# A gated convolution block on one core: order of the opening changed, and one transpose for the last 32 channels of four tiles

## What is computed

```python
xn = srms(x)                          # x over its root mean square, by pixel
u = silu(xn @ u_w.T + u_b)            # 288 channels
v = silu(xn @ v_w.T + v_b)            # 288 channels
# a[288 channels, 128 offsets]: two small networks (3 layers of 256) of the offset
out = toeplitz_columns(v, a2) + toeplitz_rows(v, a1)    # in the reference by FFT
return (u * out) @ o_w.T + o_b + x
```

## Time and profile before

| | us |
|---|---|
| median of 3 runs | 752.12 |
| the three runs | 749.59, 752.12, 756.20 |
| the profiled execution | 749.46 |
| its span, first to last instruction | 747.7 |
| phase A, to | 148 |
| C0, to | 295 |
| body0, to | 507 |
| C1, to | 645 |
| body1, to | 748 |

### The profile page before, as it was taken

The page is one execution under the profiler, slowest core; times in us unless marked ns, Lnnn a source line. Parts: engine busy times, 40 slices in busy tenths (PEclk is TensorE's granted clock), DMA queues, the critical chain, the costliest instruction groups (busy, mean ns, idle before and its releaser), DMA issues.

```text
span 747.7 us, 19150 instructions
## 1 busy us (share of the span) xinstructions
PE 725.0 (97%) x7190; PEld 671.3 (90%) x7190; DVE 479.3 (64%) x863; ACT 528.3 (71%) x862; POOL 275.8 (37%) x184
## 2 busy tenths in 40 slices
PE   6899999999999998999999999999999999999998
PEld 6899899999999998899999999998999999887886
DVE  8477756258989898454444455445545455888887
ACT  4566678867767675778777778775767767676775
POOL 3233343112111213555554555511000000598984
PEclk9999999999999999999999999999999999999999
DMA  8755565499889985688888888869564656699996
GB/s 201 199 170 170 170 175 178 173 260 208 170 200 201 199 197 180 186 282 265 264 271 270 265 284 263 271 209 219 134 157 118 157 126 135 209 298 322 334 333 198
DMA packets 132308, 161.15 MB, mean 216 GB/s; under 512 B 69772, under 2 KB 97420, under 8 KB 132236
## 3 DMA queue, kind: packets, MB, share of 16 engines
q1 hardware_dynamic: 131948, 160.15, 76.6%
q10 hardware_dynamic: 288, 0.00, 0.0%
HBM read 109.49 MB, written 50.63 MB: 214 GB/s over the span
## 4 chain that ended last, share of the span: by engine, by line
PE 83%; DVE 8%; DMA 5%; issue 2%; SPq 1%; ACT 1%; POOL 0%; DVEq 0%; POOLq 0%; ACTq 0%
PE ps L1055 23%; PE ps L1162 17%; PE ps L1078 10%; PE ps L1068 10%; PE ps L1147 9%; PE ps L1134 8%; PE ps L1044 3%; DMA x_e<-in_x_eT 3%; PE ps L1081 2%; DVE toepB L903 2%; DMA free_rows<-in_x 1%; DVE r_diag L756 1%; DMA stage<-a_dram 1%; PE ps L1023 1%; DVE n_tmp L724 1%
## 5 line engine op out<-in xcount | busy, mean ns | idle before, releaser
L541 POOL TENSOR_TENSOR u_in<-u_in,v 128x1152 f32<-128x1152 f32 (+2 forms) x67 | 175.0, 2622 | 139.4 <-DMA u_in<-u_dram 132.2
L954 DVE TENSOR_TENSOR g<-ps,g 128x512 fp32r<-128x512 f32 (+1 forms) x192 | 125.4, 680 | 45.2 <-ACT g L614 42.2
L1162 PE MATMUL ps<-toepB,vt 128*128 128x128 f32 x1152 | 138.6, 278 | 0.2 <-DVE toepB L903 0.2
L1162 PEld LDWEIGHTS ps<-toepB,vt 128*128 128x128 f32 x1152 | 131.5, 192 | 6.8 <-ACT vt L650 6.1
L903 DVE COPY toepB<-stage 64x512 f32<-64x512 f32 x144 | 108.9, 756 | 43.4 <-PE ps L1162 40.1
L1055 PE MATMUL ps<-wv,xh 97*128 97x288 f32 x512 | 118.4, 307 | 5.4 <-DVE xl L811 5.2
L1055 PE MATMUL ps<-wu,xh 97*128 97x288 f32 x512 | 121.9, 303 | 0.0
L811 DVE TENSOR_TENSOR xl<-ps,xh 96x512 fp32r<-96x512 f32 x64 | 43.6, 682 | 108.5 <-ACT xh L586 108.4
L1068 PE MATMUL ps<-ident,u_in 128*128 128x128 f32 (+1 forms) x768 | 99.7, 272 | 3.1 <-DVE g L954 1.7
L1078 PE MATMUL ps<-g,wo 128*96 128x512 f32 x384 | 101.9, 400 | 0.0
L590 ACT ACTIVATE v<-ps 128x576 f32<-128x576 f32 (+1 forms) x128 | 83.4, 652 | 22.8 <-PE ps L1055 10.0
(11 more groups left out here) (84 smaller groups left out, 1015.4 us busy)
## 6 DMA issues: line engine op xcount, KB each, us to landing
stage<-a_dram SPq DMA_DIRECT2D x144, 256.0 KB, 4.6
u_in<-u_dram SPq DMA_DIRECT2D x64, 576.0 KB, 5.3
u_dram<-u_out SPq DMA_DIRECT2D x48, 576.0 KB, 3.3
x_e<-in_x_eT SPq DMA_DIRECT2D x64, 192.0 KB, 4.2
out<-x_e SPq DMA_DIRECT2D x64, 192.0 KB, 3.9
u_dram<-u_in SPq DMA_DIRECT2D x16, 576.0 KB, 2.9
x_n<-in_x SPq DMA_DIRECT2D x16, 384.0 KB, 5.8
xa<-in_x SPq DMA_DIRECT2D x64, 96.0 KB, 4.5
```

The lines of the kernel that those rows point to most:

```text
L541: return nc.gpsimd.tensor_tensor(out=tile, in0=tile, in1=v[:, start // 2:end // 2, bass.ds(t * NB, NB)].rearrange("p c n e -> p n c e"), o ...
L954: nc.vector.tensor_tensor(out=low, in0=ps[0:w, bank], in1=high.bitcast(f32), op=ALU.subtract).then_inc(gl_ready, 1)
L1162: last = nc.tensor.matmul(ps[:, SET_BANK[n % 2] + c // NB, (c % NB) * P:(c % NB + 1) * P], vt[n % 2][:, c], toepB[half][n % 2][:, c], star ...
```

## The change

1. **Opening.** ACT: `high_x(0, 0)` goes ahead of the squares of chunk 1. DVE: `low_x(1, 1)` goes ahead of the sum of chunk 1's squares. POOL: in the first chunk all four squares of chunk 2 are issued in step 3 (before: one in step 2, three in step 3).
2. **Networks.** PE issues `rpe_spreads` behind pair 3 of step 2 instead of behind pair 1.
3. **Joints.** DVE: `set_x_rows(0)` two units earlier. PE: in step 0 of body0 pair 2 ahead of the transposes of block 2. SP: at the end of body0 `load_xe` ahead of `load_stage`.
4. **body0, block 2.** POOL gates channels 0 to 255 in place and the last 32 of all four tiles into a new tile u_rest [128 tokens, 4 x 32], in a second instruction. PE transposes u_rest at once: one transpose 128x128, whose row is 32 n + channel. ACT copies the four groups of 32 rows to rows 0 to 31 of g[:, 4], each into its tile's columns (4 x 32x128); DVE copies each to rows 64 to 95 and subtracts into rows 32 to 63 (8 x 32x128). L1081 waits for all of it by two more semaphores. Half 1 keeps the old way.

The core of the diff:

```diff
@@ sync, body of phase_b0 @@
-                        if t >= STEPS - 2:
-
-                            sp.wait_ge(y_transposed, NCH * t)
-                            load_stage(1, t - (STEPS - 2))
                         if not first or r >= 2:
                             sp.wait_ge(o_stored[0][r % 2], 32 * c + 16 * (r // 2))
                             load_xe(0, t, r)
+                        if t >= STEPS - 2:
+
+                            sp.wait_ge(y_transposed, NCH * t)
+                            load_stage(1, t - (STEPS - 2))
@@ gpsimd @@
-                        for k in (((), (), (0,), (1, 2, 3)) if first else ((), (0,), (1,), (2, 3)))[r]:
+                        for k in (((), (), (), (0, 1, 2, 3)) if first else ((), (0,), (1,), (2, 3)))[r]:
                             square_a0(c + 2, k)
...
+                target = tile
+                if half == 0 and start == EARLY:
+                    target = u_rest[:, r % CH].rearrange("p (n c e) -> p n c e", n=NB, e=2)
...
-                        gate(0, t + 1, r + 1, c + 1 + (r + 1) // CH).then_inc(ug_ready, 1)
+                        loads = c + 1 + (r + 1) // CH
+                        gate(0, t + 1, r + 1, loads, 0, EARLY)
+                        gate(0, t + 1, r + 1, loads, EARLY, D).then_inc(ug_ready, 1)
@@ scalar @@
+            def high_rest(t, bank):
+
+                act.wait_ge(y_transposed, NCH * t + NCH)
+                wait(act, o_projected, t)
+                for n in range(NB):
+                    nc.scalar.copy(tile_columns(g[0:KW[2], 4], n), rest_of(ps[:, bank], n)).then_inc(gh_ready, 1)
+
...
+            high_x(0, 0)
             squares_of(x_chunk(1), x_sq1[:], 1)
-            high_x(0, 0)
@@ vector @@
+            low_x(1, 1)
             dve.wait_ge(opening_squared, 2)
             sum_opening(CH, CH, x_sq1[:])
-            low_x(1, 1)
...
-                    if half == 0 and n == UNITS - 1:
+                    if half == 0 and n == UNITS - 3:
                         set_x_rows(0)
...
+            def low_rest(t, bank):
+
+                w = KW[2]
+                for n in range(NB):
+                    dve.wait_ge(gh_ready, (2 + NB) * t + 2 + n + 1)
+                    nc.vector.tensor_copy(tile_columns(g[2 * w:3 * w, 4], n), rest_of(ps[:, bank], n)).then_inc(g_second, 1)
+                    low = nc.vector.tensor_tensor(out=tile_columns(g[w:2 * w, 4], n), in0=rest_of(ps[:, bank], n),
+                                                  in1=tile_columns(g[0:w, 4], n).bitcast(f32), op=ALU.subtract)
+                    low.then_inc(gl_ready if n == NB - 1 else g_low, 1)
@@ tensor @@
+                if half == 0 and k == NCH - 1:
+
+                    nc.tensor.transpose(ps[:, bank, 0:P], u_rest[:, r % CH], ident[:]).then_inc(y_transposed, 1)
+                    return
...
+                        if half == 0:
+                            pe.wait_ge(g_second, NB * (m + 1))
+                            pe.wait_ge(g_low, (NB - 1) * (m + 1))
                         nc.tensor.matmul(ps[0:E, bank], wo[0:REST + 2, 4], tile[0:REST + 2, 4],
...
-                if c <= LAYERS and r == 2:
-                    rpe_spreads(c)
...
+                    if c <= LAYERS and r == 2:
+                        rpe_spreads(c)
...
+                    if start:
+                        project(1, xs, r, 2)
                     transpose_g(0, t, r, 2, banks[2], NCH * t + 1)
-                    project(1, xs, r, 2)
+                    if not start:
+                        project(1, xs, r, 2)
```

More of the change, by code:

```diff
@@ L165, in tno_kernel, with rest_of, tile_columns @@
         assert base + K + 8832 <= nc.sbuf_usable_end
+        def rest_of(source, n):
+            return source[KW[2] * n:KW[2] * (n + 1), 0:P].rearrange("p (i c) -> p i c", i=2)
+        def tile_columns(rows, n):
+            return rows.rearrange("p (s i q c) -> p s q i c", s=2, i=2, q=2)[:, n // 2, n % 2]
         def u_tile(half, r):
@@ L412, in body @@
                             load_xa(t + 3, r + 1)
+                        if not first or r >= 2:
+                            sp.wait_ge(o_stored[0][r % 2], 32 * c + 16 * (r // 2))
+                            load_xe(0, t, r)
                         if t >= STEPS - 2:
@@ L540, in gate @@
                 tile = u_in[:, r % CH, :, start:end].rearrange("p n (c e) -> p n c e", e=2)
+                target = tile
+                if half == 0 and start == EARLY:
+                    target = u_rest[:, r % CH].rearrange("p (n c e) -> p n c e", n=NB, e=2)
                 return nc.gpsimd.tensor_tensor(
-                    out=tile, in0=tile, in1=v[:, start // 2:end // 2, bass.ds(t * NB, NB)].rearrange("p c n e -> p n c e"),
+                    out=target, in0=tile, in1=v[:, start // 2:end // 2, bass.ds(t * NB, NB)].rearrange("p c n e -> p n c e"),
                     op=ALU.mult)
@@ L689, in body0 @@
                             silu_v(1, t, pair)
-                    high_g(t, 2, banks[2], g, t)
+                    high_rest(t, banks[2])
                     for pair in range(2):
@@ L946, in set_rows, with gh_before, low_g @@
                     nc.vector.memset(tile[REST:REST + 2, 4].bitcast(f32), 1.0).then_inc(g_rows_set, 1)
-            def low_g(m, k, bank, tile):
-                dve.wait_ge(gh_ready, (NCH + 1) * m + (k + 1 if k < 2 else k + 2))
+            def gh_before(half, t):
+                return (2 + NB) * (t if half == 0 else STEPS) + (NCH + 1) * (t if half else 0)
+            def low_rest(t, bank):
[6 more added lines that the diff above has]
+                    low.then_inc(gl_ready if n == NB - 1 else g_low, 1)
+            def low_g(half, t, k, bank, tile):
+                dve.wait_ge(gh_ready, gh_before(half, t) + (k + 1 if k < 2 else k + 2))
                 w = KW[k]
@@ L1069, in transpose_g, with project_out @@
                 last.then_inc(y_transposed, 1)
-            def project_out(m, tile, bank, free, which=range(NCH)):
+            def project_out(half, m, tile, bank, free, which=range(NCH)):
                 for k in which:
@@ L1214, in body0 @@
                         pe.wait_ge(wo_split, 6)
-                    project_out(t, g, O_BANK, t, range(2))
+                    project_out(0, t, g, O_BANK, t, range(2))
                     project(1, xs, r, 3)
-                    project_out(t, g, O_BANK, t, (2,))
+                    project_out(0, t, g, O_BANK, t, (2,))
             def body1(c, first, last):
@@ L1231, in body1 @@
                     if not (first and r == 0):
-                        project_out(STEPS + t - 1, g1[(r + 1) % 2], 6 + (r + 1) % 2, 0 if first and r < 3 else STEPS + t - 2)
+                        project_out(1, STEPS + t - 1, g1[(r + 1) % 2], 6 + (r + 1) % 2, 0 if first and r < 3 else STEPS + t - 2)
             phase_c(0)
@@ L1237, in _ @@
             chunks(pe, body1)
-            project_out(ALL_STEPS - 1, g1[1], 7, ALL_STEPS - 2)
+            project_out(1, ALL_STEPS - 1, g1[1], 7, ALL_STEPS - 2)
 def kernel(**inputs):
```

13 lines of the change are left out of this document (6 added, 7 removed).

## The result

The changed kernel is slower: 764.17 us in the median of six runs (763.03 to 767.92) beside 751.61 for the kernel before; the ratio is 1.0175, 95% interval 1.0138 to 1.0212. A second set of runs of the same code gave 764.91 beside 752.30 (1.0165, 1.0130 to 1.0200). The forecast was 755, the range ended at 764; the measured median stands at its upper end, just outside.

What follows compares the result with a forecast made beforehand. PE was taken to bound body0, until DVE's longer chain held it. The terms +8.7 - 1.4 - 2.7 - 0.4 - 0.35 = +3.85 us gave 753.3 on the profiled execution, 756.0 on the median; forecast 755, range 743 to 764.

Steps and rivals of the forecast that it cites:

- The chain of eight: In body0, eight DVE operations one after another delay L1081: each step 0.29 us longer, to 6.85, +8.7 us in all.
- the recorded sum: In body0, with the skill's formula (an estimated 291 ns an operation), the sum was put at +10.6 us instead of +8.7.
- The two waits added on PE end with the chain above: Before body0's late product, PE's two new waits were said to end with DVE's chain, with no cost of their own.
- Part 4: Joint to body0: -0.4 us (0 to -1.3), of which 0.2 from moving the memsets; pair 2 fills a wait of 1.37.
- Part 2: Opening: reordered work lets PE start at 19.3 and 24.9, -1.4 us (-1.1 to -1.6).
- What is late next: Opening: after GpSimd's earlier scaling, DVE's xl of step 2 holds PE to 24.9, not 23: -1.6 us at most.
- Part 3: rpe_spreads after pairs 2 and 3: two products cover each of three r_diag waits of some 0.93, -2.7 us (-2.4 to -2.8).
- Part 5: Joint behind body0: x_e's earlier load removes a wait, but toepB's corners leave 0.38 at most; -0.35 us (0 to -1.5).
- only the silu binds: Rival for body0: DVE's small operations overlap or are shorter, -3.3 us there, -8.2 in all, 743 us; chance 0.13.

Runs made afterwards that it cites:

- experiment 4: Changed kernel with DVE's four copies replaced by one ACT copy of 32x512 inside g: 746.05 us, ratio 0.9899.
- experiment 3: Changed kernel with DVE's ten operations a step counted on one semaphore, the two added PE waits gone: 764.08 us, run again 761.21 beside the changed kernel's 764.91.
- experiment 2: Changed kernel with body0 written out as 32 steps on PE alone, other engines keeping their loops: 761.12 us, ratio 1.0102.
- experiment 5: Memsets back behind the last unit: changed kernel without block 2, 748.37 us; changed kernel with ACT's copy, 745.00. Kernel before with the spreads' move alone: 748.76.
- Experiment 6: Kernel before with the opening's three order changes alone: 751.71 us. Experiment 5's kernel with ACT's copy, SP's first u stores ahead of chunk 3's load: 742.14.

## Why the prediction was wrong, point by point

- **The chain of eight, right.** An operation took 0.287 (forecast 0.28), the gap 0.03 (0.03), ACT's piece 0.25 (0.27), and a step outside the loop 6.86 to 6.90 (6.85). The Trainium skill (VectorE: DVE Perf Modes, "Two Vector instructions with no wait between them") holds every one of them, and the trace agrees: no pair overlaps, in the four of experiment 4 neither, whose outputs stay in one group of partitions while their inputs change it. The same page's formula, which it gives for an fp32 addition of two tensors at 512 and 2048 columns, makes an estimated 0.291 for 128; the measured 0.286 lies between it and the interpolation. With it the recorded sum would be +11.3, not the +10.6 written there: 8 x 0.011 more than 0.29 a step, over 30 steps.
- **"The two waits added on PE end with the chain above": the step that failed.** They were costed at nothing because all three conditions hold at the same moment, and the loop of PE's queue wasn't priced at all. But in the loop the two waits hold PE after the chain has ended: 3.7 to 3.9 us in experiment 3. With the loop's turns, 0.3 to 0.5 us each, the loop cost 4.9 in all (experiment 2). The slack of 0.70 in the earlier trace rows had covered the turns before. Written out, the two waits did cost nothing, as forecast. The forecast took the reaction of PE from one written-out row of the opening, 0.06, and allowed 0.10; inside the loop it was 0.23.
- The rest of `body0`'s miss: 213.94 - 202.98 = 11.0 with the loop written out, against 8.7. Most of its steps took 6.90 to 6.94, 0.07 above the forecast's 6.85; over 30 steps that is 2.1. Of these 0.07, 0.02 show outside the loop too (6.87); the rest isn't explained.
- **Part 4, "I take 0.2, between 0 and the whole 0.96": wrong in sign.** This is the second step that failed: the joint got 2.7 us longer (experiment 5). The argument asked only whether DVE had idle time for the memsets, not what they would push where. The profile of before shows the price, in rows that weren't read: an operation of 128x16 took 0.69 beside a scaling of x at the joint, and earlier in C0 one took 2.62:

```profile
183.55 2.75 POOL L488 TENSOR_TENSOR x_n<-x_n 128x1536 f32<-128x1536 f32 x1 [8.33 <-DMA x_n<-in_x]
183.71 2.62 DVE L725 TENSOR_SCALAR n_tmp<-n_tmp 128x16 f32<-128x16 f32 x1
```

  Pair 2's move ahead of the transposes gave nothing that can be told from this.
- **Part 2, the opening: both starts right, the gain none.** "What is late next" was asked once, for DVE, and not once more: behind it stood ACT's silu of step 2, pinned by SP's store at 31.86 and 31.96. Experiment 6's profiles show it: at an undisturbed clock the row sums come at the same time with either order. That the second execution's opening is 1.3 us shorter, as forecast, is luck: the kernel before had 3 us of half clock in its profile (39.67, where the old order without it opens at 38.4 to 38.5).
- **Part 3, the spreads: right, mis-sized.** -3.5 us in the trace and alone (752.30 to 748.76), against -2.7: 1.1 to 1.2 for each of the three, where a wait of 0.93 had been counted. The cover held; no wait stands before their matmuls.
- **Part 5: the mechanism right, the size inside its bounds (-0.7 and -0.8; 0 to -1.5), what makes it not shown.** The wait for x_e is gone, and the second unit's column product starts 4.0 us behind the last late product instead of 5.4; then its rows wait for POOL's corners, as forecast. But from the last late product to those rows it is 7.4 to 7.6 in the three profiles of the changed kernel and its unrolled form, 7.85 and 8.49 with one semaphore, 8.63 in the kernel of block 2 alone, whose late product is late as well but whose load has the old place, and 8.25 to 9.52 with the new place and no lateness (8.32 before). Neither the load's place nor the lateness is thus shown to shorten it by itself.
- **The rival "only the silu binds"** had the right number for the step, 6.45, and stood on the wrong condition: it came true not with shorter operations but with four of them taken from DVE (experiment 4).

The second execution of the changed kernel adds up within its trace: -1.3 - 3.5 + 2.7 + 15.9 - 0.8 + 0.3 = +13.3 on the span, and 761.0 - 747.7 = 13.3. The medians of that set differ by 12.6.

## What to carry to other kernels

In a hardware loop, more waits on PE's queue and the loop's turn cost nothing here as long as PE came to them 0.7 us or more behind its inputs, and 0.17 us and 0.3 to 0.5 us once it stood at them. So when a change makes PE wait in a loop, price the added waits and the turn by themselves, and try one semaphore counted up by all producers instead of three; written out, the same waits cost nothing. And before a short operation of DVE is moved, look which instruction of POOL runs at its new place and at the place of what it pushes; before a stall is booked as gained, follow every engine to its next wait for something that hasn't moved, SP's stores included.

## What the runs showed of the hardware

- Two waits more on PE's queue, against values from registers, cost 0.17 us a step where PE stood at them (0.23 from DVE's end to PE's start instead of 0.06), and a loop's turn 0.3 to 0.5; against constants, in written-out steps, they cost nothing (0.05 to 0.06 with three waits as with one). With PE 0.7 us behind its inputs both cost nothing in the loop either.
- An operation of DVE on 128x16 took 2.27 us beside a gate of POOL (128x1024, 2.4 to 2.7 us) and 0.75 beside squares of 128x384, instead of 0.17 to 0.18, and ended 0.03 behind POOL's. The Trainium skill (SBUF — State Buffer, "SBUF: two separate sides") has DVE and GpSimd share a pair of ports by an exclusive lock, and has the one that comes second blocked for the other's whole instruction; the trace agrees, to the end of the instruction. Operations with one input were held as those with two (the one in the kernel of the spreads alone). DVE's subtractions with one input in PSUM were not: in a step of the changed kernel two of 128x512 took their usual 1.27 together (369.82 to 371.09) beside a gate that ran from 368.31 to 370.75.
- PE's clock fell to its lower level (granted 0.50, 1.2 GHz of 2.4) near the opening at different places in executions of one code: at 34 to 37 us in the first profile, at 25 to 28 in the second, and not at all from 13 to 38 us in the kernel with PE's loop written out, whose opening is the same; in four other kernels with the new order it was 0.50 from 13 up to 19 to 22.5 us and again for some 3 us from 29 on. In the first profile:

```profile
34.00:37.00 3.00, 3.00 (x17) 3.00 (x16) 0.34 (x1) 0.71 (x2) 0.00 (x0) 0.50 0.48 195
```

  What PE did before: it had stood 2.34 us before 32.76 there. In the second execution it had stood 1.63 before 24.82.
